# Causal mask of the attention numerators moved from VectorE to ScalarE and GpSimd

## The chip, the cores and the metric

One Trainium2 chip; the kernel runs on one of its NeuronCores. The metric is the device time of one execution in microseconds (us). Every time below is in us from the start of the profiled span unless it says otherwise.

## What is computed

The whole kernel is one decoder block over 16 sequences of 224 tokens with 512 channels: causal self-attention with a rational softmax, cross-attention, and a mixture of experts. The change touches the self-attention alone, of which the reference computes, for 16 heads of 32 channels:

```
scores = q @ k.T * scale - |t - s| * slope[head]
scores = where(s > t, -10000, scores)
num    = 0.5 * (1 + scores * rsqrt(1 + scores * scores))
probs  = num / (sum(num) + 1e-6)
out    = probs @ v
x      = x + out @ w_out.T
```

## The kernel before

Three stages run one after the other: `self_attention`, `cross_attention`, `experts`. Each has its own block in which the five engines (TensorE is `pe`, VectorE `dve`, ScalarE `act`, GpSimd `pool`, SyncE `sp`) run their own instruction lists, held together by semaphores. A stage starts when the one before it has ended on all engines.

`self_attention` works in 8 iterations `i` over two sequences each. An iteration has 8 steps `s`; a step handles four heads of one sequence. The first, the second and the last iteration have bodies of their own ("first", "second", "last"); iterations 2 to 6 are five passes of one loop ("mid"). The order of the work in a step is written out by hand, and so is the table `PLAN` of other products (query, key and value projections Q, K, V of the next sequences, transposes T, output projection OUT, the query projection Z of the next stage) that fill TensorE in each step. The attention itself is pipelined over the steps. In step `s`:

- TensorE issues `scores(s+1)` (L666, L670, L674: four heads, 336 columns each, into the PSUM tile `sc`), then `values(s)` (L691, L694: numerators times v, and numerators times ones, into `pv`), then the step's products. `values(s)` waits for `diag_made`, `off_made` and, as `pv` has one buffer, for `o_made` of the step before.
- ScalarE makes the high part of the last output (`hi_of_output`, L529), then for step `s+1` the square of the scores (L510), the reciprocal root r (L512) and r squared (L514), then the reciprocal of the denominator of step `s` (L522, L524), then copies products out of PSUM, in steps 1 and 2 also normalises 512-channel rows (L476, four instructions), and then `off_diagonal(s+1)` (L518).
- VectorE makes, in this order, the low part of the last output (L383), `product_signed(s+1)` (L360: scores times r), `numerator(s+1)` (L364, L367 and, so far, L369) and `output(s)` (L375, L376, L378, which makes `o_made`), with residual sums and statistics in between.

The numerators of a step lie as four heads by 336 columns on 112 partitions: columns 0 to 223 are the two diagonal blocks (112 keys by 112 queries each), columns 224 to 335 the block below the diagonal, which needs no mask. L367 leaves y there, and the numerator (but for a constant factor) is 2 - y. ScalarE makes 2 - y of the last 112 columns of each head (L518, 448 elements a partition). VectorE makes it of the first 224 (L369, 896 elements) and masks at once, as (y - 2) * keep, where `keep` holds -1 where the query is not before the key and 0 elsewhere:

```
dve.wait_ge(y_made, i * NG + n + 1)
dve.scalar_tensor_tensor(num[n % 2][:, :, 0:2 * R], num[n % 2][:, :, 0:2 * R], 2.0,
                         keep[:, None, :].broadcast_to([R, 4, 2 * R]), ALU.subtract, ALU.mult).then_inc(diag_made, 1)
```

GpSimd fills constants at the start of the stage, `keep` among them, and has nothing to do in it after that. `num` has two buffers.

Of the kernel before, what the change touches and what calls it, by code (L numbers as in the profile page):

```python
# [25 lines left out]
def self_attention(nc, x, w_qkvT, w_outT, w_qT, slopes, x1_dram, q2_dram):  # L26
# [7 lines left out]
    with ExitStack() as ctx:  # L34
# [7 lines left out]
        keep = sb("keep", [R, 2 * R])  # L42
# [63 lines left out]
        diag_made, off_made = sem("diag_made"), sem("off_made")  # L106
        pv_full, rs_made, rden_made, d_made, o_made = sem("pv_full"), sem("rs_made"), sem("rden_made"), sem("d_made"), sem("o_made")
# [78 lines left out]
        CONSTS = 6  # L186
# [69 lines left out]
        def _(pool):  # L256
            pool.memset(ident[:], 1.0).then_inc(const_set, 1)
            pool.memset(keep[:], -1.0).then_inc(const_set, 1)
# [9 lines left out]
            pool.wait_ge(const_set, 11)  # L268
# [3 lines left out]
            for a in range(2):  # L272
                pool.affine_select(out=keep[:, a * R:a * R + R], in_=keep[:, a * R:a * R + R], pattern=[[1, R]],
                                   compare_op=ALU.is_ge, fill=0.0, base=0, channel_multiplier=-1).then_inc(const_ready, 1)
            pool.affine_select(out=head_sel[:], in_=head_sel[:], pattern=[[-6, 4], [-32, 4]], compare_op=ALU.is_ge, fill=0.0,
                               base=0, channel_multiplier=1).then_inc(const_ready, 1)
            pool.wait_ge(const_ready, 4)
# [4 lines left out]
                               base=0, channel_multiplier=1).then_inc(const_ready, 1)  # L282

        @block.vector
        def _(dve):
# [76 lines left out]
            def numerator(i, n):  # L362
                dve.wait_ge(rr_made, i * NG + n + 1)
                dve.scalar_tensor_tensor(u_sb, u_sb, 1.0, q_sb, ALU.add, ALU.mult).then_inc(m_made, 1)  # L364
                dve.wait_ge(p_made, i * NG + n + 1)
                dve.wait_ge(m_made, i * NG + n + 1)
                dve.scalar_tensor_tensor(num[n % 2], u_sb, 3.0, num[n % 2], ALU.subtract, ALU.mult).then_inc(y_made, 1)  # L367
                dve.wait_ge(y_made, i * NG + n + 1)
                dve.scalar_tensor_tensor(num[n % 2][:, :, 0:2 * R], num[n % 2][:, :, 0:2 * R], 2.0,  # L369
                                         keep[:, None, :].broadcast_to([R, 4, 2 * R]), ALU.subtract, ALU.mult).then_inc(diag_made, 1)  # L370
# [97 lines left out]
        def _(act):  # L468
# [47 lines left out]
            def off_diagonal(i, n):  # L516
                act.wait_ge(y_made, i * NG + n + 1)
                act.activation(num[n % 2][:, :, 2 * R:], num[n % 2][:, :, 2 * R:], ACT.Copy, bias=2.0, scale=-1.0).then_inc(off_made, 1)  # L518
# [77 lines left out]
        def _(pe):  # L596
# [81 lines left out]
            def values(i, n):  # L678
                b, g = divmod(n, 4)
                pe.wait_ge(diag_made, i * NG + n + 1)  # L680
                pe.wait_ge(off_made, i * NG + n + 1)
                if not (isinstance(i, int) and i * NG + n == 0):
                    pe.wait_ge(o_made, i * NG + n)
                for den in range(2):
                    for st in range(2):
                        for r in range(4):
                            h = 4 * g + r
                            lhs = ones[:] if den else v[:, 2 * b + st, 32 * h:32 * h + 32]
                            o0 = den * T
                            if st == 0:  # L690
                                mm = pe.matmul(pv[32 * r:32 * r + 32, o0:o0 + T], lhs, num[n % 2][:, r, R:NPAIR],  # L691
                                               start=True, stop=False, tile_position=(0, 32 * r))
                            else:
                                mm = pe.matmul(pv[32 * r:32 * r + 32, o0 + R:o0 + T], lhs, num[n % 2][:, r, 0:R],  # L694
                                               start=False, stop=True, tile_position=(0, 32 * r))
                mm.then_inc(pv_full, 1)
# [1079 lines left out]
```

## Time and profile before

| | us |
|---|---|
| median of 3 runs (lowest, highest) | 3380.05 (3374.13, 3383.58) |
| the profiled execution, its own time | 3391.78 |
| its span, first to last instruction | 3390.1 |
| TensorE busy in the span | 3071.0 (91%) |
| VectorE busy | 1669.1 (49%) |
| ScalarE busy | 1351.4 (40%) |
| GpSimd busy | 732.2 (22%) |
| mean granted TensorE clock | 0.951 |

The profile is of one execution. It took 11.7 us longer than the median run, 1.68 us of which lie around the span. Busy shares are means over three stages with different limits, so they say little on one stage.

### The profile page before, as it was taken

Reading aid. Unit: us, or ns where it says so; the run is one execution under the profiler, and the core shown is the slowest. Engines: PE = TensorE matmul, PEld = TensorE weight load, DVE = VectorE, ACT = ScalarE, POOL = GpSimd, SP = SyncE. Lnnn points to the kernel's source line nnn. Section 1 sums busy time; section 2 is a strip of 40 time slices with the busy share of each in tenths; the row PEclk is TensorE's granted clock in tenths of the full one; section 3 lists DMA queues with packets and bytes.
Section 4 is the critical chain, followed back from the end, with each engine's and each line's share of the span. In section 5 each row is a group of like instructions: output and inputs, shape, how many; then the busy total and the mean of one; then the engine's idle time right before and its main releaser. Section 6 shows DMA issues by size and latency. Waiting matters only on the chain. (4 is left out here: it accounts for less than half of the span.)

```text
span 3390.1 us, 52927 instructions
## 1 busy us (share of the span) xinstructions
PE 3071.0 (91%) x19340; PEld 2500.3 (74%) x19340; DVE 1669.1 (49%) x3816; ACT 1351.4 (40%) x2297; POOL 732.2 (22%) x564
## 2 busy tenths in 40 slices
PE   5889999865999999999999839999999999999997
PEld 4667777754777777777777628887888788878886
DVE  5888888843555565555555623232223232323232
ACT  5677777743555555555555411111111111111111
POOL 0000000001112222121221123333333333333333
PEclk9889999977999999999999859999999999999999
DMA  2011111114111111111110022222222222222222
GB/s 95 23 34 44 43 43 43 44 50 145 37 37 43 36 51 52 36 37 42 48 54 23 17 70 72 61 83 70 74 61 83 70 74 63 81 72 72 66 78 59
DMA packets 96191, 193.80 MB, mean 57 GB/s; under 512 B 18656, under 2 KB 28640, under 8 KB 94016
## 3 DMA queue, kind: packets, MB, share of 16 engines
q1 hardware_dynamic: 80912, 160.78, 15.6%
q0 software_dynamic: 15152, 31.26, 4.4%
q8 instruction: 88, 1.44, 0.2%
q14 instruction: 39, 0.32, 0.0%
HBM read 144.19 MB, written 47.82 MB: 57 GB/s over the span
## 5 line engine op out<-in xcount | busy, mean ns | idle before, releaser
L1619 DVE CAST f_hh<-f_hf 128x448 fp32r<-128x448 f32 x256 | 116.8, 456 | 893.2 <-ACT f_hf L1643 860.5
L1643 ACT ACTIVATE f_hf<-f_h 128x448 f32<-128x448 f32 x256 | 139.6, 545 | 1016.0 <-PE f_h L1679 983.2
L1566 POOL TENSOR_TENSOR f_w1l<-f_raw,f_w1h 128x512 fp32r<-128x512 f32 x130 | 183.4, 1411 | 829.2 <-DVE f_w1h L1601 829.1
L1695 PE MATMUL f_y<-f_w2h,f_hh 128*128 128x512 f32 x896 | 357.9, 399 | 0.0
L1695 PE MATMUL f_y<-f_w2h,f_hl 128*128 128x512 f32 x896 | 354.0, 395 | 0.0
L1695 PE MATMUL f_y<-f_w2l,f_hh 128*128 128x512 f32 x896 | 352.3, 393 | 0.0
L1266 ACT ACTIVATE c_s_sb<-c_s_sb,c_nmx 112x750 f32<-112x750 f32 x256 | 236.0, 922 | 188.9 <-DVE c_nmx L1095 186.5
L1679 PE MATMUL f_h<-f_xTh,f_w1h 128*128 128x448 f32 x1024 | 261.8, 378 | 32.3 <-ACT f_hf L1643 16.8
L1258 ACT COPY c_pT<-c_psum 125x672 f32<-125x672 f32 x256 | 184.7, 722 | 241.1 <-PE c_psum L1359 237.4
L1359 PEld LDWEIGHTS c_psum<-c_ident,c_s_sb 112*125 112x125 f32 x1536 | 198.2, 194 | 90.2 <-issue 84.5
L1679 PE MATMUL f_h<-f_xTl,f_w1h 128*128 128x448 f32 x1024 | 256.1, 373 | 0.0
L1679 PEld LDWEIGHTS f_h<-f_xTh,f_w1h 128*128 128x128 f32 x1024 | 187.9, 190 | 91.0 <-issue 28.2
L1679 PE MATMUL f_h<-f_xTh,f_w1l 128*128 128x448 f32 x1024 | 253.5, 369 | 0.0
L1091 DVE CUSTOM_DVE_ANT_0 c_s_sb<-c_psum,c_mb 112x750 f32<-112x750 f32 x256 | 238.4, 931 | 9.4 <-PE c_psum L1350 9.4
L1359 PE MATMUL c_psum<-c_ident,c_s_sb 112*125 112x112 f32 x1536 | 227.8, 286 | 9.9 <-ACT c_pT L1258 9.3
L1350 PE MATMUL c_psum<-c_kT,c_q 64*112 64x376 f32 x1024 | 207.6, 526 | 21.4 <-DVE c_mx L1091 19.2
L1679 PEld LDWEIGHTS f_h<-f_xTl,f_w1h 128*128 128x128 f32 x1024 | 196.8, 192 | 17.4
L1679 PEld LDWEIGHTS f_h<-f_xTh,f_w1l 128*128 128x128 f32 x1024 | 196.6, 192 | 17.4
L1695 PEld LDWEIGHTS f_y<-f_w2h,f_hl 128*128 128x128 f32 x896 | 168.2, 188 | 39.4
L1695 PEld LDWEIGHTS f_y<-f_w2l,f_hh 128*128 128x128 f32 x896 | 169.0, 189 | 29.7
L1695 PEld LDWEIGHTS f_y<-f_w2h,f_hh 128*128 128x128 f32 x896 | 168.3, 188 | 29.6
L1571 POOL TENSOR_TENSOR f_w2l<-f_raw,f_w2h 128x512 fp32r<-128x512 f32 x130 | 169.9, 1307 | 35.0 <-ACT f_ys L1651 35.0
(243 smaller groups left out, 5725.5 us busy)
## 6 DMA issues: line engine op xcount, KB each, us to landing
f_raw<-in_w SPq DMA_DIRECT2D x132, 512.0 KB
c_craw<-in_ctxT SPq DMA_DIRECT2D x16, 1125.0 KB, 5.1
a_x_in<-in_x SPq DMA_DIRECT2D x9, 896.0 KB, 5.7
a_xr<-in_x SPq DMA_DIRECT2D x8, 896.0 KB, 6.0
x_dram<-a_xr SPq DMA_DIRECT2D x8, 896.0 KB, 4.8
q_dram<-a_q SPq DMA_DIRECT2D x32, 224.0 KB, 5.3
c_q<-q_dram SPq DMA_DIRECT2D x16, 448.0 KB, 5.5
c_x<-x_dram SPq DMA_DIRECT2D x16, 448.0 KB, 4.6
```

Of the source, the lines that this page charges most:

```text
L1091: nc.vector.tensor_tensor_reduce(out=half(s_sb[:, h % 4, :]), in0=score_view(h), in1=half(mb[:]), scale=1.0, scalar=-FLT_MAX, op0=ALU.add, ...
L1258: act.copy(probs_view(h), pt_view).then_inc(p_copied, 1)
L1266: act.activation(s_sb[:, h % 4, :], s_sb[:, h % 4, :], ACT.Exp, bias=nmx[:, h:h + 1], accum_out=den[:, h:h + 1]).then_inc(e_made, 1)
L1350: mm = pe.matmul(scb[e][0:R, a, 0:HW], q[rows, m, t0:t0 + R], kT[rows, m, j0:j0 + HW], start=True, stop=True, tile_position=(64 * e, 0))
L1359: mm = pe.transpose(ptb[0:JB, 128 * j:128 * j + R], s_sb[:, h % 4, JB * j:JB * j + JB], ident[:])
L1566: pool.tensor_tensor(w1s[1][:, n % NSLOT].rearrange("p k c -> p (k c)"), raw1[:, g % 2, n % 2, :], w1s[0][:, n % NSLOT].rearrange("p k c - ...
L1571: pool.tensor_tensor(w2s[1][:, n % NSLOT], raw2[:, g % 2, n % 2, :], w2s[0][:, n % NSLOT].bitcast(F32), ALU.subtract).then_inc(w_lo, 1)
L1619: dve.tensor_copy(hs[0][:, l % 2, c * HC:c * HC + HC], hf[:, c, :]).then_inc(h_hi, 1)
L1643: act.activation(hf[:, c, :], H[:, 0:HC], ACT.Gelu_apprx_tanh).then_inc(free, 1)
L1679: mm = pe.matmul(H[:, 0:HC], w1s[a][:, l % NSLOT, k, :], xT[p][b][:, k, c * HC:c * HC + HC], start=q + k == 0, stop=(q, k) == (2, KC - 1))
L1695: mm = pe.matmul(Y[t][:], hs[a][:, l % 2, 128 * t:128 * t + 128], w2s[b][:, l % NSLOT, :], start=j == 0 and q == 0, stop=j == FB - 1 and q ...
```

## The change

ScalarE makes 2 - y of all columns: `off_diagonal` gets a second instruction ahead of the old one, over the 896 elements of the two diagonal blocks, which raises the new semaphore `two_made`. GpSimd then masks in place, with one affine selection for each diagonal block (448 elements a partition: four heads by 112 queries; entries where the query index is below the partition's key index become 0), and each raises `diag_made`. `values` waits for both. VectorE's L369, with its wait for `y_made`, the tile `keep` and its three set-up instructions on GpSimd are gone. GpSimd also raises a semaphore `two_seen` that nobody waits for.

```diff
-            pool.memset(keep[:], -1.0).then_inc(const_set, 1)
...
-            for a in range(2):
-                pool.affine_select(out=keep[:, a * R:a * R + R], in_=keep[:, a * R:a * R + R], pattern=[[1, R]],
-                                   compare_op=ALU.is_ge, fill=0.0, base=0, channel_multiplier=-1).then_inc(const_ready, 1)
...
+            def diagonal(i, n):
+                pool.wait_ge(two_made, i * NG + n + 1)
+                pool.sem_inc(two_seen, 1)
+                for a in range(2):
+                    block_a = num[n % 2][:, :, a * R:a * R + R]
+                    pool.affine_select(out=block_a, in_=block_a, pattern=[[0, 4], [1, R]], compare_op=ALU.is_ge, fill=0.0,
+                                       base=0, channel_multiplier=-1).then_inc(diag_made, 1)
+
+            diagonal(0, 0)
+
+            def body(i, kind):
+                for s in range(NG):
+                    if has_step(kind, s + 1):
+                        diagonal(*step(i, s + 1))
+
+            iterations(pool, body)
...
                 dve.scalar_tensor_tensor(num[n % 2], u_sb, 3.0, num[n % 2], ALU.subtract, ALU.mult).then_inc(y_made, 1)
-                dve.wait_ge(y_made, i * NG + n + 1)
-                dve.scalar_tensor_tensor(num[n % 2][:, :, 0:2 * R], num[n % 2][:, :, 0:2 * R], 2.0,
-                                         keep[:, None, :].broadcast_to([R, 4, 2 * R]), ALU.subtract, ALU.mult).then_inc(diag_made, 1)
...
             def off_diagonal(i, n):
                 act.wait_ge(y_made, i * NG + n + 1)
+                act.activation(num[n % 2][:, :, 0:2 * R], num[n % 2][:, :, 0:2 * R], ACT.Copy, bias=2.0, scale=-1.0).then_inc(two_made, 1)
                 act.activation(num[n % 2][:, :, 2 * R:], num[n % 2][:, :, 2 * R:], ACT.Copy, bias=2.0, scale=-1.0).then_inc(off_made, 1)
...
-                pe.wait_ge(diag_made, i * NG + n + 1)
+                pe.wait_ge(diag_made, i * (2 * NG) + 2 * n + 2)
```

## Rows read from the trace of the kernel before

**Rows 1.** Windows, stages 1 and 3: length, busy of PE, PEld, DVE, ACT, POOL, clock.

```profile
0.00:767.00 767.00, 637.89 (x5504) 497.87 (x5504) 580.33 (x865) 509.77 (x733) 3.23 (x21) 0.92 0.16 47
...
2000.00:3390.00 1390.00, 1317.86 (x6012) 1112.71 (x6012) 408.78 (x831) 220.28 (x379) 488.95 (x374) 0.98 0.26 71
```

**Rows 2.** Waits from 160 to 720: who waited for whom, total, times, longest.

```profile
DVE a_ew L360 <- ACT a_ew L512: 76.5, 47, 2.3
...
PE a_pv L691 <- DVE a_o_sb L378: 43.2, 17, 7.6
...
PE a_pv L691 <- ACT a_ew L518: 18.3, 6, 3.0
```

**Rows 3.** Timeline of ScalarE and VectorE, step 4 of a mid iteration: start, duration.

```profile
435.52 0.38 ACT L529 CAST a_oTh<-a_o_sb 128x224 fp32r<-128x224 f32 x1 [1.57 <-DVE a_o_sb L378]
...
438.57 1.56 DVE L360 TENSOR_TENSOR a_ew<-a_sc,a_ew 112x1344 f32<-112x1344 f32 x1 [2.25 <-ACT a_ew L512]
...
443.29 0.58 ACT L518 ACTIVATE a_ew<-a_ew 112x448 f32<-112x448 f32 x1 [1.10 <-DVE a_ew L367]
...
443.29 1.09 DVE L369 SCALAR_TENSOR_TENSOR a_ew<-a_ew,a_keep 112x896 f32<-112x896 f32 x1
...
445.44 0.38 ACT L529 CAST a_oTh<-a_o_sb 128x224 fp32r<-128x224 f32 x1 [1.57 <-DVE a_o_sb L378]
```

**Rows 4.** Groups of ScalarE from 80 to 980: busy, mean ns of one.

```profile
L514 ACT ACTIVATE a_ew<-a_ew 112x1344 f32<-112x1344 f32 x61 | 81.1, 1329 | 1.9
...
L518 ACT ACTIVATE a_ew<-a_ew 112x448 f32<-112x448 f32 x61 | 35.1, 576 | 40.5 <-DVE a_ew L367 40.1
```

**Rows 5.** Groups of GpSimd over the whole span.

```profile
L1571 POOL TENSOR_TENSOR f_w2l<-f_raw,f_w2h 128x512 fp32r<-128x512 f32 x130 | 169.9, 1307 | 35.0 <-ACT f_ys L1651 35.0
...
L273 POOL TENSOR_SCALAR_AFFINE_SELECT a_keep<-a_keep 112x112 f32<-112x112 f32 x2 | 0.5, 278 | 0.0
...
L1549 POOL TENSOR_SCALAR_AFFINE_SELECT f_ident<-f_ident 128x128 f32<-128x128 f32 x1 | 0.3, 299 | 0.1
...
L275 POOL TENSOR_SCALAR_AFFINE_SELECT a_head_sel<-a_head_sel 128x16 f32<-128x16 f32 x1 | 0.2, 219 | 0.0
```

**Rows 6.** Timeline of ScalarE, steps 1 to 3 of the same mid iteration.

```profile
413.42 0.56 ACT L518 ACTIVATE a_ew<-a_ew 112x448 f32<-112x448 f32 x1
...
421.89 0.55 ACT L503 ACTIVATE a_q<-a_gen 128x448 f32<-128x448 f32 x1 [1.05 <-PE a_gen L601]
...
425.15 0.56 ACT L518 ACTIVATE a_ew<-a_ew 112x448 f32<-112x448 f32 x1
425.62 0.36 ACT L529 CAST a_oTh<-a_o_sb 128x224 fp32r<-128x224 f32 x1
```

**Rows 7.** Timeline of TensorE, from step 2 of that iteration; in brackets idle before.

```profile
413.56 0.60 PE L620 MATMUL a_tb<-a_ident,a_x_in 112*128 112x112 f32 x4 [0.75 <-ACT a_x_in L476]
...
415.01 0.58 PE L691 MATMUL a_pv<-a_ew,a_v 112*32 112x224 f32 x8
...
425.82 0.98 PE L691 MATMUL a_pv<-a_ew,a_v 112*32 112x224 f32 x8 [3.04 <-ACT a_ew L518]
...
435.63 0.81 PE L691 MATMUL a_pv<-a_ew,a_v 112*32 112x224 f32 x8 [3.01 <-DVE a_o_sb L378]
...
445.55 0.59 PE L691 MATMUL a_pv<-a_ew,a_v 112*32 112x224 f32 x8 [0.28 <-DVE a_o_sb L378]
...
497.98 0.60 PE L620 MATMUL a_tb<-a_ident,a_x_in 112*128 112x112 f32 x4 [0.75 <-ACT a_x_in L476]
```

**Rows 8.** Timeline of TensorE in the first iteration.

```profile
88.74 0.97 PE L691 MATMUL a_pv<-a_ew,a_v 112*32 112x224 f32 x8 [4.38 <-DVE a_o_sb L378]
...
108.58 0.58 PE L691 MATMUL a_pv<-a_ew,a_v 112*32 112x224 f32 x8 [1.52 <-DVE a_o_sb L378]
```

**Rows 9.** Timeline of VectorE and GpSimd in the experts' stage.

```profile
2207.33 2.14 DVE L1619 CAST f_hh<-f_hf 128x448 fp32r<-128x448 f32 x1 [4.02 <-ACT f_hf L1643]
2207.36 1.85 POOL L1571 TENSOR_TENSOR f_w2l<-f_raw,f_w2h 128x512 fp32r<-128x512 f32 x1
```

More of the change, by code:

```diff
@@ L41, in self_attention @@
         ident = sb("ident", [R, R])
-        keep = sb("keep", [R, 2 * R])
         ones = sb("ones", [R, 32])
@@ L106, in self_attention @@
         diag_made, off_made = sem("diag_made"), sem("off_made")
+        two_made, two_seen = sem("two_made"), sem("two_seen")
         pv_full, rs_made, rden_made, d_made, o_made = sem("pv_full"), sem("rs_made"), sem("rden_made"), sem("d_made"), sem("o_made")
@@ L185, in self_attention @@
         stage = lambda n: ew[:, n * 3 * C:(n + 1) * 3 * C]
-        CONSTS = 6
+        CONSTS = 4
         block = ctx.enter_context(nc.Block())
@@ L267, in _ @@
             pool.iota(s_iota, [[1, R]], base=0, channel_multiplier=0, allow_small_or_imprecise_dtypes=True).then_inc(const_set, 1)
-            pool.wait_ge(const_set, 11)
+            pool.wait_ge(const_set, 10)
             pool.affine_select(out=ident[:], in_=ident[:], pattern=[[1, R]], compare_op=ALU.is_equal, fill=0.0,
                                base=0, channel_multiplier=-1).then_inc(const_ready, 1)
-            for a in range(2):
-                pool.affine_select(out=keep[:, a * R:a * R + R], in_=keep[:, a * R:a * R + R], pattern=[[1, R]],
-                                   compare_op=ALU.is_ge, fill=0.0, base=0, channel_multiplier=-1).then_inc(const_ready, 1)
             pool.affine_select(out=head_sel[:], in_=head_sel[:], pattern=[[-6, 4], [-32, 4]], compare_op=ALU.is_ge, fill=0.0,
                                base=0, channel_multiplier=1).then_inc(const_ready, 1)
-            pool.wait_ge(const_ready, 4)
+            pool.wait_ge(const_ready, 2)
             pool.affine_select(out=head_sel[:], in_=head_sel[:], pattern=[[6, 4], [32, 4]], compare_op=ALU.is_ge, fill=0.0,
```

## Prediction

> **What bounds the kernel now.** I read the windows of the three stages first [rows 1]. The change lies in the first, 767 of 3390 us. TensorE is busy for 638 of these, more than VectorE (580) and ScalarE (510), and GpSimd does nothing after its constants. No engine is full, so the order of the work decides. The list of waits says how [rows 2]: VectorE waits for ScalarE's reciprocal root in 47 steps, TensorE waits for VectorE's output (`o_made`) 17 times, 43.2 us, and for ScalarE's L518 six times, 18.3 us. So there are two kinds of wait, and the timeline of one mid iteration shows where each stands.
>
> *The loop between ScalarE and VectorE.* L529 at 435.52 is followed by the square, the root, VectorE's L360, L364 and L367. y is there at 443.29, 7.77 after L529. L518 and L369 start together, then comes `output`, and the next L529 starts at 445.44 [rows 3]. One turn is 9.92 us, of which 2.15 lie between y and L529.
>
> *TensorE.* In the mid iteration `values` waits 3.04, 3.01 and 0.28 us, and from 445.55 TensorE has no idle until the transposes at 497.98, which wait 0.75 for the normalised rows [rows 7]. So over 52 us of an iteration of 84.4 (413.56 to 497.98) TensorE alone sets the pace. The wait of 3.04 is of another kind than the loop: TensorE's Z product ends, ScalarE copies it out (421.89), normalises four rows of blocks, and only then comes L518 (425.15), though y has long been there [rows 6]. `values` starts at 425.82, behind L518. Here ScalarE's queue lies on TensorE's path.
>
> **The change, part by part.**
>
> *Removed.* L369, 1.09 us of VectorE in each of 64 steps. `output` could start right after L367. On GpSimd's set-up three instructions of 0.2 to 0.3 us go; nobody waits for them. VectorE sets the end in none of TensorE's 52 us, so nothing comes back there.
>
> *Added on ScalarE.* 896 elements. L514 takes 1329 ns for 1344 elements, L518 576 ns for 448 [rows 4]: (1329 - 576) / 896 = 0.84 ns an element, so 576 + 448 * 0.84 = 0.95 us. Neighbours on ScalarE overlap by 0.1 (425.15 to 425.62 for 0.56, [rows 6]), so it lengthens the queue by 0.85. It goes ahead of the old L518.
>
> *Added on GpSimd.* Two selections of 448 elements, of which the trace has no like. From 16 elements (219 ns) to 112 (278) is 0.61 ns an element, from 112 to 128 (299) is 1.3 [rows 5]. These give 0.48 and 0.72 us for 448. From above, four selections of 112 are 1.11 and a two-input subtraction of 512 takes 1.31. I take 0.65 each, 1.3 for the pair (0.96 to 2.25), as it is nearest to the selections of the same engine and inner length, with something for the three more rows of the pattern. To this come 0.1 from ScalarE to GpSimd and 0.1 to TensorE, my estimate from the 0.1 between y's maker and the start of its readers and between L518 and `values` (425.71 to 425.82).
>
> The GPSIMD Engine Reference of the Trainium skill (section 4.1) has it that one-input work on GpSimd goes at roughly line rate, and section 3.1 gives 1.8 cycles an element for a tight loop. By my estimate from that page 448 elements are then 0.4 to 0.7 us, and the sum would stay near what the rows give.
>
> *A new turn of the loop.* y at 7.77 after L529. Then ScalarE has 0.85 for the new instruction and 0.47 for L518: the next L529 comes 9.09 after the last. By VectorE alone it would be 9.92 - 1.01 = 8.91 (L369 overlaps its neighbour by 0.08), so ScalarE decides. A turn gains 0.83. But the masked columns are there 7.77 + 0.95 + 0.1 + 1.3 + 0.1 = 10.2 after L529, where `values` now starts 10.1 after it (445.55 for 435.52). So `values` no longer hangs on `o_made` but on GpSimd: it gains nothing in the first turn and 0.83 in each one that follows.
>
> *A mid iteration, steps 2 to 5.* `values` of these steps starts at 415.01, 425.82, 435.63 and 445.55 [rows 7]. The anchor is TensorE's own pace up to step 2.
>
> 1. Step 2. L518 stood at 413.42, right behind a normalisation [rows 6]. The new instruction ends at 414.37, the selections at 415.8 with their waits. `values`, now at 415.01 without idle, starts 0.8 later. Queued behind it is the Z product.
> 2. Step 3. ScalarE's copy of Z (421.89) and the second normalisation come 0.8 later. The new instruction takes L518's place at 425.95, L529 comes at 427.27 instead of 425.62 (+1.65), `values` at 425.95 + 0.95 + 1.5 = 428.4 instead of 425.82 (+2.6).
> 3. Step 4, a loop turn. L529 at 436.36 (before 435.52, +0.84), `values` at 427.27 + 10.2 = 437.5 (+1.9).
> 4. Step 5. `values` at 436.36 + 10.2 = 446.56 (before 445.55): +1.0. TensorE worked 9.92 - 0.28 = 9.64 from 435.63 to 445.55 [rows 7]; with that it would be 437.5 + 9.64 = 447.1, +1.6. In this pass it ran part of it slowly: behind each idle of 3 us the first eight matmuls of `values` take 0.98 and 0.81 us instead of 0.58 [rows 7].
>
> From 445.55 TensorE has no idle, so what is lost is not made up. I take +1.3 a pass, the middle of 1.0 and 1.6. In TensorE's own steps (52.4 us for five, 10.5 each) the square starts as soon as the scores are there, just ahead of `values`, and the masked columns follow 10.2 - 0.3 = 9.9 later (the square starts 0.3 after L529). So 0.6 covers the longer path. With a pair over 1.9 `values` would be late there too, but once a pass and not in each step, since `num` has two buffers and the scores don't wait for `values`. Five passes: +6.5.
>
> *First iteration.* `values` at 88.74 waits 4.38, at 108.58 still 1.52 [rows 8], and between them lie two turns. The first gains nothing (+0.1), the next two 0.83 each: -1.5. After that TensorE sets the pace and the gain stays. *Second:* the delay of step 2 (+0.8), a normalisation behind it that TensorE doesn't wait for, and a turn or two at 0.83, -0.1. *Last:* the normalisation of step 2 and two Z products ahead of the new instruction, +1.8 at its worst by the same walk, then turns that take 0.83 off each, -0.3. Sum: 6.5 - 1.5 - 0.1 - 0.3 = **+4.6, say +5 us**, all in the first stage; the others start when it ends.
>
> *GpSimd beside VectorE.* The trace has a VectorE cast of 0.4 us that took 2.14 beside a GpSimd subtraction and ended 0.26 after it [rows 9]. If VectorE's L383 (two inputs in SBUF), 0.4 after L529's start, is held in that manner until the pair has ended, it is delayed by 0.8. L360 comes 3.05 after L529, behind an idle of 2.25 [rows 3]. I cost it at nothing; that idle is the cover, and without it the loop would grow by up to 0.8 a turn.
>
> SBUF — State Buffer of the Trainium skill, section "Who interferes with whom", speaks against the change: a VectorE instruction with two SBUF inputs and a GpSimd instruction that reads SBUF exclude each other for a whole instruction, whichever starts first. By that rule, the trace agrees, for a cast (2.14 instead of 0.4).
>
> **The rivals.**
>
> 1. *The loop sets the stage (faster).* For: 9.92 us turns and 43 us of waits for `o_made` [rows 2, 3]. If TensorE followed, each of the 26 turns of 9.89 to 9.97 us that the timeline has ([rows 3] is one) would give 0.83: -22 us, 3358. Against: the 52 us without idle, and ScalarE's queue behind the normalisations [rows 6, 7]. It decides where TensorE's apparent work is elastic (the ends of its matmuls are modelled), so that half of these turns count. The chance of more than -10 is 0.11.
> 2. *GpSimd is slow (slower).* Place: between the new ScalarE instruction and `values`. A pair of 2.25 adds 0.95 twice a pass, in step 2, which ScalarE's queue hands on, and in step 5: 5 * 1.9 = 9.5, and some 0.9 in each of the other three iterations: +17 in all, 3397. With +1.6 instead of +1.3 a pass it is +18. It decides over +10, that is from a pair of about 1.7 us, 0.86 a selection. Nothing in the trace excludes it. Chance 0.22.
> 3. *VectorE holds GpSimd (slower, smaller).* If L383 (0.4) slips between the two selections, the pair is 0.4 longer: 5 * 0.8 + 3 * 0.4 = +5 more, about +10, 3390. Against: in rows 9 it is VectorE that is held. Chance 0.12, half of it beyond +10. The page named above, of the Trainium skill, would allow either order.
>
> **How the numbers follow.** The sum stands on the profiled execution, 3391.8, and would make it 3396. The runs' median is 3380.05, 11.7 lower, and other executions should be shifted by the same 5 us: **3385**. Forecast 0.55; rivals 0.11, 0.22, 0.12. Low end: a pair of 0.96 takes 0.34 off 13 times, +0.2, and the clock can give or take about 1.2 a pass (0.4 us for each of the first three of the four groups of `values`, [rows 7]), -6: 3374. High end: rival 2 at +18 and most of such a loss, +4: 3402. 0.3% (10 us) is about what a measurement of this kernel can tell from no change. Faster by more 0.11; within it 0.55 + 0.06 = 0.61; slower by more 0.22 + 0.06 = 0.28.
>
> **What would show it.** Right: mean of the new ScalarE instruction near 0.95 us and of a selection near 0.65; turns of L529 in the first iteration near 9.1; `values` waiting for GpSimd in steps 2 to 5 of a mid iteration; TensorE's idle before `values` of step 3 near 4.7 instead of 3.0; a pass of 85.7 instead of 84.4; stages two and three as long as before. Wrong: selections under 0.5 or over 0.9 us, L367 or L364 longer than 1.56 beside GpSimd, a TensorE idle inside the 52 us, or a pass shorter than 84.

## The result, and the profile after

The changed kernel takes 3388.29 us (median, 3384.45 to 3393.59 of 13 runs), the kernel before beside it on the same chip 3381.76 (3374.13 to 3389.11, 13 runs). The ratio is 1.002, with a 95% interval of 1.0011 to 1.0029: 3.7 to 9.8 us slower. The forecast was +5, 3385 against a range of 3374 to 3402. By the prediction's bound of 0.3% this is no change, though the interval lies above one. Measured again, beside E5 and E6, the same two kernels gave 1.0017 (1.0008 to 1.0026).

The windows of stages one and three in the profile after, with the columns of [rows 1]:

```profile
0.00:767.00 767.00, 635.24 (x5504) 490.27 (x5504) 520.33 (x801) 558.29 (x796) 74.93 (x146) 0.92 0.16 47
...
2000.00:3380.00 1380.00, 1318.16 (x6004) 1113.33 (x6004) 414.44 (x830) 218.94 (x378) 482.92 (x368) 0.98 0.25 70
```

In stage one VectorE's busy time fell by 60 us, ScalarE's rose by 48.5 and GpSimd's by 72. TensorE's is nearly the same (635.24 for 637.89; stage one of the changed kernel ends 3.5 us behind this window). The waits between 160 and 720:

```profile
POOL a_ew L285 <- ACT a_ew L528: 498.8, 53, 12.0
DVE a_ew L373 <- ACT a_ew L522: 88.5, 49, 2.4
...
PE a_pv L702 <- POOL a_ew L285: 69.8, 29, 7.2
DVE a_oTl L393 <- ACT a_oTh L540: 44.3, 28, 3.3
```

L702 is `values` (L691 before), L285 the selections, L528 ScalarE's new instruction, L529 the old `off_diagonal` (L518 before), L540 `hi_of_output` (L529 before), L393 the low part of the output (L383 before). The two rows of [rows 2] in which TensorE waits for `o_made` (43.2 us) and for L518 (18.3), 61.5 together, have become one: it waits for GpSimd 29 times, 69.8 us. The groups of the moved work between 80 and 980:

```profile
L285 POOL TENSOR_SCALAR_AFFINE_SELECT a_ew<-a_ew 112x448 f32<-112x448 f32 x122 | 69.1, 590 | 572.0 <-ACT a_ew L528 572.0
...
L528 ACT ACTIVATE a_ew<-a_ew 112x896 f32<-112x896 f32 x61 | 57.9, 950 | 40.6 <-DVE a_ew L380 40.6
...
L529 ACT ACTIVATE a_ew<-a_ew 112x448 f32<-112x448 f32 x61 | 34.3, 563 | 0.0
...
L393 DVE TENSOR_TENSOR a_oTl<-a_o_sb,a_oTh 128x224 fp32r<-128x224 f32 x62 | 29.9, 483 | 46.2 <-ACT a_oTh L540 45.1 <-issue 1.1
```

ScalarE's instruction is the 950 ns of the forecast; a selection takes 590 ns instead of 650. The mid iteration that answers to [rows 3, 6, 7], steps 2 to 5, on TensorE, ScalarE, GpSimd and VectorE (x8 stands for eight matmuls, x2 for a pair of selections):

```profile
412.67 0.93 ACT L528 ACTIVATE a_ew<-a_ew 112x896 f32<-112x896 f32 x1
...
412.82 0.60 PE L631 MATMUL a_tb<-a_ident,a_x_in 112*128 112x112 f32 x4 [0.71 <-ACT a_x_in L486]
...
413.77 1.11 POOL L285 TENSOR_SCALAR_AFFINE_SELECT a_ew<-a_ew 112x448 f32<-112x448 f32 x2 [12.00 <-ACT a_ew L528]
...
414.94 0.59 PE L702 MATMUL a_pv<-a_ew,a_v 112*32 112x224 f32 x8 [0.60 <-POOL a_ew L285]
...
421.78 0.54 ACT L513 ACTIVATE a_q<-a_gen 128x448 f32<-128x448 f32 x1 [0.92 <-PE a_gen L612]
...
425.04 0.94 ACT L528 ACTIVATE a_ew<-a_ew 112x896 f32<-112x896 f32 x1
...
426.14 1.12 POOL L285 TENSOR_SCALAR_AFFINE_SELECT a_ew<-a_ew 112x448 f32<-112x448 f32 x2 [11.25 <-ACT a_ew L528]
...
426.35 0.36 ACT L540 CAST a_oTh<-a_o_sb 128x224 fp32r<-128x224 f32 x1
...
426.74 0.76 DVE L393 TENSOR_TENSOR a_oTl<-a_o_sb,a_oTh 128x224 fp32r<-128x224 f32 x1 [2.57 <-ACT a_oTh L540]
...
427.31 0.98 PE L702 MATMUL a_pv<-a_ew,a_v 112*32 112x224 f32 x8 [4.65 <-POOL a_ew L285]
...
435.83 0.38 ACT L540 CAST a_oTh<-a_o_sb 128x224 fp32r<-128x224 f32 x1
...
436.81 0.58 PE L702 MATMUL a_pv<-a_ew,a_v 112*32 112x224 f32 x8 [1.96 <-POOL a_ew L285]
...
443.60 0.95 ACT L528 ACTIVATE a_ew<-a_ew 112x896 f32<-112x896 f32 x1 [1.78 <-DVE a_ew L380]
...
444.92 0.36 ACT L540 CAST a_oTh<-a_o_sb 128x224 fp32r<-128x224 f32 x1
...
445.88 0.58 PE L702 MATMUL a_pv<-a_ew,a_v 112*32 112x224 f32 x8 [1.03 <-POOL a_ew L285]
```

To compare kernels, count from the transposes L631 (L620 before) of the same pass, at 412.82 here and 413.56 before. `values` of steps 2, 3, 4 and 5 starts 2.12, 14.49, 23.99 and 33.06 us after them; before it was 1.45, 12.26, 22.07 and 31.99. So step 2 is 0.67 late, step 3 2.23, step 4 1.92, step 5 1.07. L540 turns in 9.48 (426.35 to 435.83) and then in 9.09 (to 444.92) where it turned in 9.92, and still `values` comes later. The turn of 9.48 is longer than the forecast 9.09 because ScalarE first waits 2.20 us for a product of TensorE that stands behind the late `values` of step 3, and copies it, before it comes to L528:

```profile
433.66 0.54 ACT L513 ACTIVATE a_q<-a_gen 128x448 f32<-128x448 f32 x1 [2.20 <-PE a_gen L612]
...
434.51 0.96 ACT L528 ACTIVATE a_ew<-a_ew 112x896 f32<-112x896 f32 x1
```

The next transposes are at 498.34 (before 497.98), so the pass takes 85.52 instead of 84.42: the 1.1 us of step 5, not made up afterwards.

### The profile page after: what moved, and what is told of

Its sections match the earlier page's. It is cut to its first block and busy times, and to the rows that moved or that the text cites. A ratio compares the mean times of both kernels' runs of the same rounds, so it can differ in the third digit from the quotient of the medians.

```text
span 3383.2 us, 53207 instructions
## 1 busy us (share of the span) xinstructions
PE 3062.8 (91%) x19340; PEld 2492.9 (74%) x19340; DVE 1616.0 (48%) x3752; ACT 1399.8 (41%) x2361; POOL 804.2 (24%) x689
## 3 DMA queue, kind: packets, MB, share of 16 engines
q0 software_dynamic: 15152, 31.26, 4.4%
q8 instruction: 88, 1.44, 0.2%
## 5 line engine op out<-in xcount | busy, mean ns | idle before, releaser
L285 POOL TENSOR_SCALAR_AFFINE_SELECT a_ew<-a_ew 112x448 f32<-112x448 f32 x128 | 72.4, 590 | 643.4 <-ACT a_ew L528 643.4
```

Of the source, the lines that this page charges most:

```text
L285: pool.affine_select(out=block_a, in_=block_a, pattern=[[0, 4], [1, R]], compare_op=ALU.is_ge, fill=0.0, base=0, channel_multiplier=-1).th ...
```

## The experiments

E1 to E4 ran together on one chip, E5 and E6 on another together with both kernels again, E7 and E8 together on a third. Each ratio is to runs of the kernel before beside the experiment; on the chip of E1 to E4 that kernel took 3400.74 us and on the others 3382 to 3383, so whole times are compared only as ratios. Stage one does carry over from chip to chip: E4 and E7, the same kernel, end it at 762.0 and 762.3. The table has `values` of steps 2 to 5 in the pass about 410, in us after the transposes, the usual length of a pass, and the end of stage one, which is the time at which GpSimd starts the next stage's constants.

| | 2 | 3 | 4 | 5 | pass | stage one | ratio (95%) |
|---|---|---|---|---|---|---|---|
| before | 1.45 | 12.26 | 22.07 | 31.99 | 84.4 | 767.5 | |
| before, again | 1.45 | 12.20 | 22.02 | 31.95 | 84.3 | 766.5 | |
| after | 2.12 | 14.49 | 23.99 | 33.06 | 85.5 | 770.5 | 1.002 (1.0011-1.0029) |
| after, again | 2.11 | 14.49 | 24.06 | 33.14 | 85.5 | 771.2 | 1.0017 (1.0008-1.0026) |
| E1, no selections | 1.45 | 13.12 | 22.37 | 31.26 | 83.7-84.3 | 761.1 | 0.9996 (0.9981-1.0011) |
| E2, only the removal | 1.45 | 12.18 | 20.87 | 29.67 | 82.0 | 742.7 | 0.9921 (0.9897-0.9944) |
| E3, only ScalarE's load | 1.45 | 13.04 | 22.85 | 32.78 | 85.0-85.2 | 772.5 | 1.0012 (0.9999-1.0026) |
| E4, steps 2, 3 on VectorE | 1.45 | 12.25 | 22.09 | 31.57 | 83.6-83.9 | 762.0 | 0.9996 (0.9981-1.0011) |
| E5, 2 - y on VectorE | 1.45 | 12.28 | 21.98 | 31.44 | 83.9 | 765.6 | 0.9995 (0.9985-1.0005) |
| E6, selections twice | 3.54 | 18.79 | 30.07 | 40.08 | 92.5-94.3 | 826.3 | 1.0183 (1.0166-1.02) |
| E7, E4 again | 1.45 | 12.17 | 22.00 | 31.58 | 83.3-84.0 | 762.3 | 0.9991 (0.9982-1.0) |
| E8, E7 in halves | 1.44 | 12.17 | 21.84 | 31.12 | 83.2-84.8 | 763.7 | 0.9977 (0.9967-0.9986) |

The end of stage one holds a spread that no kernel here explains: E6 apart, TensorE reaches its first `values` between 52.6 and 54.2 us. Counted from there, stage one takes 714.6 and 713.6 us before, 717.4 in both profiles after, and 709.4 and 709.6 in E4 and E7.

**E1. The change without the selections.** The mask is left out.

```diff
-                for a in range(2):
-                    block_a = num[n % 2][:, :, a * R:a * R + R]
-                    pool.affine_select(...).then_inc(diag_made, 1)
...
-                pe.wait_ge(diag_made, i * (2 * NG) + 2 * n + 2)
+                pe.wait_ge(two_made, i * NG + n + 1)
```

> The changed kernel without the two selections (the mask is left out, so later keys count too); TensorE waits for ScalarE's new instruction in their place. Marks, in us after the transposes of normalised rows in a mid pass: values of steps 2, 3, 4, 5 now at 2.12, 14.49, 23.99, 33.06, pass 85.5, first stage ends at 770.5. Theory (TensorE hangs on ScalarE's new instruction and then on GpSimd's pair, each added once in step 2 and once in step 5): step 2 back to 1.45, step 3 at 13.0, step 5 at 31.2, pass 83.7, stage end near 760. Rival (ScalarE's longer queue alone makes the loss, the selections lie beside other work): pass 85 or more, stage end at 769 to 771.

The timeline of TensorE in E1, steps 3 to 5, from its transposes at 408.91:

```profile
422.03 0.98 PE L698 MATMUL a_pv<-a_ew,a_v 112*32 112x224 f32 x8 [3.88 <-ACT a_ew L525]
...
431.28 0.58 PE L698 MATMUL a_pv<-a_ew,a_v 112*32 112x224 f32 x8 [1.67 <-ACT a_ew L525]
...
440.17 0.58 PE L698 MATMUL a_pv<-a_ew,a_v 112*32 112x224 f32 x8 [0.84 <-ACT a_ew L525]
```

TensorE waits for ScalarE's second instruction (L525, the old `off_diagonal` behind the new one). Step 3 is still 0.86 later than before, step 5 0.73 sooner. The selections with their hand-overs are the rest: 1.37 in step 3 (14.49 - 13.12), 1.62 and 1.80 in steps 4 and 5. The pass is 1.2 to 1.8 shorter than after, the stage 9 us (761.1 for the expected 760), so the rival, which had the selections lie beside other work, fell. The whole run shows nothing that its interval can tell from one, so this experiment stands on the passes.

**E2. Only the removal.** The kernel before without L369; 2 - y and the mask of the first 224 columns of each head are left out.

```diff
-                dve.wait_ge(y_made, i * NG + n + 1)
-                dve.scalar_tensor_tensor(num[n % 2][:, :, 0:2 * R], num[n % 2][:, :, 0:2 * R], 2.0,
-                                         keep[:, None, :].broadcast_to([R, 4, 2 * R]), ALU.subtract, ALU.mult).then_inc(diag_made, 1)
...
-                pe.wait_ge(diag_made, i * NG + n + 1)
+                pe.wait_ge(y_made, i * NG + n + 1)
```

> The kernel before without VectorE's mask instruction and with nothing in its place (the 896 elements stay y, unmasked): what the removal alone gives. Theory (the loop gains 1.0 a turn, but step 3 hangs on ScalarE's queue and the steps from 5 on are TensorE's own): step 3 unchanged at 12.26, step 5 at 30 to 30.7 instead of 31.99, pass 82.4 to 83.1 instead of 84.4, stage end near 752 instead of 767.5. Rival (the removal is hidden, TensorE sets the pace everywhere): pass 84.4, stage end 767. Rival (the loop sets the stage): 26 turns and all steps shorter, more than 26 us, stage end below 742.

The timeline of TensorE in E2, from the transposes at 399.21:

```profile
411.39 0.58 PE L688 MATMUL a_pv<-a_ew,a_v 112*32 112x224 f32 x8 [3.04 <-ACT a_ew L515]
...
420.08 0.59 PE L688 MATMUL a_pv<-a_ew,a_v 112*32 112x224 f32 x8 [1.85 <-DVE a_o_sb L375]
...
428.88 0.59 PE L688 MATMUL a_pv<-a_ew,a_v 112*32 112x224 f32 x8 [0.77 <-DVE a_o_sb L375]
```

From `values` to `values` it is 8.80 us (428.88 - 420.08), 1.1 less than before. Step 3 doesn't move (12.18), as it hangs on ScalarE's queue and not on VectorE; steps 4 and 5 gain 1.2 and 2.3. The pass is 2.4 shorter, and the stage 25 us. That is more than I had expected (a pass of 82.4 or more, an end near 752) and hardly short of the 742 at which the rival, the loop that sets the stage, was to be taken as true. It isn't by the rival's way, though: step 3 doesn't move, and from step 5 to the next transposes it is 52.3 us as before (82.0 - 29.67; 84.42 - 31.99 = 52.4). The rest lies outside the later mid passes: the second iteration, 79.9 from transposes to transposes where it was 83.6, gains more than a mid pass. The whole run is 22 us shorter (3378.59 for 3400.74, by the interval 19 to 35). So L369's time is worth much in this stage, if nothing takes its place. With the mask gone the later stages work on other data, which may bear on the whole run and doesn't on the passes.

**E3. Only ScalarE's load.** The kernel before, with the new instruction writing its 896 elements into a spare tile.

```diff
                 act.wait_ge(y_made, i * NG + n + 1)
+                act.activation(q_sb[:, :, 0:2 * R], r_sb[:, :, 0:2 * R], ACT.Copy, bias=2.0, scale=-1.0)
                 act.activation(num[n % 2][:, :, 2 * R:], num[n % 2][:, :, 2 * R:], ACT.Copy, bias=2.0, scale=-1.0).then_inc(off_made, 1)
```

> The kernel before with one more ScalarE instruction of 896 elements ahead of the old one, into a tile that is dead by then; its result is not used. VectorE still masks. Theory (ScalarE's queue behind the normalisations is on TensorE's path): steps 3, 4, 5 later by 0.85 each (13.1, 22.9, 32.8), pass 85.2 instead of 84.4, stage end near 772; loop turns stay at 9.92. Rival (GpSimd alone makes the loss): pass 84.4, stage end 767.5.

As expected: 0.78 us later in step 3 and no more in steps 4 and 5, and the pass 0.6 to 0.8 longer. The idle ahead of step 3 grows from 3.04 [rows 7] to 3.88, in E1 too:

```profile
428.77 0.97 PE L692 MATMUL a_pv<-a_ew,a_v 112*32 112x224 f32 x8 [3.88 <-ACT a_ew L519]
```

The queue behind the normalisation is a cost on its own, paid once a pass, and the stage is 5 us longer (1.1 of them ahead of the first `values`). The whole run's interval, 0.9999 to 1.0026, just holds one. The first mid pass is an exception: it takes 85.06 us here and 86.01 in the kernel before, for which see the part on the sum.

**E4. The other version.** VectorE keeps the masking in steps 2 and 3, where ScalarE has a normalisation ahead; the other six steps are as changed. The edit against the changed kernel, in the lists of GpSimd, VectorE and ScalarE (the counts that GpSimd and TensorE wait for change with it):

```diff
+        ON_DVE = (2, 3)
...
+                if n in ON_DVE:
+                    return
...
+                if n in ON_DVE:
+                    dve.wait_ge(y_made, i * NG + n + 1)
+                    dve.scalar_tensor_tensor(num[n % 2][:, :, 0:2 * R], num[n % 2][:, :, 0:2 * R], 2.0,
+                                             keep[:, None, :].broadcast_to([R, 4, 2 * R]), ALU.subtract, ALU.mult).then_inc(diag_dve, 1)
...
-                act.activation(num[n % 2][:, :, 0:2 * R], ...).then_inc(two_made, 1)
+                if n not in ON_DVE:
+                    act.activation(num[n % 2][:, :, 0:2 * R], ...).then_inc(two_made, 1)
```

> The changed kernel, but the numerators of steps 2 and 3 of each iteration, which stand behind the normalisations in ScalarE's queue, are masked by VectorE as before. Theory: steps 2 and 3 back at 1.45 and 12.26, step 4 at 22.1, step 5 at 31.2 to 31.8 (before 31.99, changed 33.06), pass 83.6 to 84.2, stage end near 762.5, which is faster than both kernels, by some 5 us against before. Rival (the loss comes in all steps alike): pass 85 or more, stage end 769 or more.

Steps 2 and 3 are back at 1.45 and 12.25, step 5 is 0.42 sooner than before, and stage one ends at 762.0, 5 us before both profiles of the kernel before and 8 to 9 before those of the changed one. The rival, a loss in all steps alike, fell. The whole run's interval (0.9981 to 1.0011) holds one, and also the 0.9985 that 5 us would make.

**E5. 2 - y of the masked columns on VectorE.** ScalarE has only its old instruction, GpSimd masks.

```diff
+                dve.wait_ge(y_made, i * NG + n + 1)
+                dve.tensor_scalar(num[n % 2][:, :, 0:2 * R], num[n % 2][:, :, 0:2 * R], -1.0, 2.0, ALU.mult, ALU.add).then_inc(two_made, 1)
...
-                act.activation(num[n % 2][:, :, 0:2 * R], num[n % 2][:, :, 0:2 * R], ACT.Copy, bias=2.0, scale=-1.0).then_inc(two_made, 1)
```

> VectorE makes 2 - y of the 896 elements without the mask (one tensor input, constants), GpSimd masks as in the changed kernel, ScalarE has its old queue again. Theory: steps 2 and 3 back at 1.45 and 12.26. If VectorE's new instruction is faster than its old one (0.62 us) and nothing holds it, a loop turn is 9.45, step 5 at 31.2, pass 83.6, stage end near 762. Rival (GpSimd's selections now run beside VectorE's output, whose last instruction reads two SBUF tiles and is held until the pair ends): a turn of about 10.1 instead of 9.92, step 5 at 32.4, pass 84.8, stage end near 770.

VectorE, and under it GpSimd, in step 5 of E5:

```profile
441.53 0.63 DVE L382 TENSOR_SCALAR a_ew<-a_ew 112x896 f32<-112x896 f32 x1
...
442.79 0.39 DVE L390 SCALAR_TENSOR_TENSOR a_o_sb<-a_dt 128x224 f32<-128x224 f32 x1
```

```profile
442.32 1.30 POOL L285 TENSOR_SCALAR_AFFINE_SELECT a_ew<-a_ew 112x448 f32<-112x448 f32 x2 [8.16 <-DVE a_ew L382]
```

And the pair of step 4 of the same pass, with each selection by itself, beside the same VectorE instruction:

```profile
433.33 0.39 DVE L390 SCALAR_TENSOR_TENSOR a_o_sb<-a_dt 128x224 f32<-128x224 f32 x1
```

```profile
432.87 0.58 POOL L285 TENSOR_SCALAR_AFFINE_SELECT a_ew<-a_ew 112x448 f32<-112x448 f32 x1 [9.41 <-DVE a_ew L382]
433.40 0.77 POOL L285 TENSOR_SCALAR_AFFINE_SELECT a_ew<-a_ew 112x448 f32<-112x448 f32 x1
```

The same 896 elements cost VectorE 0.63 us here and 1.09 in L369 [rows 3], which also reads `keep`. Step 3 is at its old place again: with ScalarE's queue untouched the delay of step 3 is gone, which is E3 the other way round. The rival (the pair holds VectorE's `output`, turns of 10.1) fell: L390, which reads two SBUF tiles, took 0.39 as ever, and it was the pair that took 1.30 instead of 1.11. The turn is the 9.45 of the theory (433.76 to 443.22 for L541, `hi_of_output`), but its sizes were missed: step 5 at 31.44 for 31.2, a pass of 83.9 for 83.6, and the stage ends at 765.6 for 762, only 1 to 2 us ahead of the kernel before. The whole run's interval holds one.

**E6. Each selection twice.** One cost doubled, the rest as changed.

```diff
-                for a in range(2):
+                for q, a in enumerate((0, 1, 0, 1)):
+                    if q == 2:
+                        pool.wait_ge(diag_made, i * (4 * NG) + 4 * n + 2)
+                        pool.sem_inc(two_seen, 1)
...
-                pe.wait_ge(diag_made, i * (2 * NG) + 2 * n + 2)
+                pe.wait_ge(diag_made, i * (4 * NG) + 4 * n + 4)
```

> The changed kernel with each pair of selections made twice (the second finds nothing left to do): the pair's time goes from 1.1 to about 2.35 us. Theory: step 2 at 3.4 instead of 2.12, step 3 at 17.0 instead of 14.49, step 5 at 35.5 instead of 33.06, pass 88.0 instead of 85.5, and in TensorE's own steps up to 0.5 more once; stage end near 786 instead of 770.5. Rival (the selections are hidden beside other work in most steps): pass under 86.5.

Step 2 came as worked out (3.54 for 3.4), the rest did not: step 3 at 18.79 for 17.0, step 5 at 40.08 for 35.5, a pass of 92.5 to 94.3 for 88.0, and stage one ends 40 us later than the 786 expected. The rival, selections that are hidden beside other work, fell. TensorE in E6, from the transposes at 439.54:

```profile
443.08 0.59 PE L705 MATMUL a_pv<-a_ew,a_v 112*32 112x224 f32 x8 [2.03 <-POOL a_ew L288]
...
458.33 0.97 PE L705 MATMUL a_pv<-a_ew,a_v 112*32 112x224 f32 x8 [5.92 <-POOL a_ew L288]
...
469.61 0.58 PE L705 MATMUL a_pv<-a_ew,a_v 112*32 112x224 f32 x8 [3.24 <-POOL a_ew L288]
```

And the windows behind steps 2 and 3 in E6, then behind the same two steps in the changed kernel; the seventh number is the granted clock:

```profile
443.00:451.40 8.40, 8.32 (x60) 6.77 (x60) 6.23 (x8) 4.59 (x7) 0.03 (x1) 0.80 0.00 0
458.30:465.40 7.10, 7.07 (x51) 5.42 (x51) 5.57 (x6) 3.17 (x5) 0.00 (x0) 0.57 0.43 132
```

```profile
414.90:421.70 6.80, 6.76 (x64) 5.67 (x64) 4.60 (x5) 5.87 (x9) 0.00 (x0) 1.00 0.00 0
427.30:433.90 6.60, 6.59 (x52) 5.04 (x52) 4.62 (x4) 4.30 (x6) 0.00 (x0) 0.63 0.62 201
```

Behind an idle of 2.03 us instead of 0.60 TensorE's work of step 2 took 1.6 us more, at a clock of 0.80 instead of 1.00. That is nearly all of the 1.8 by which step 3 missed its 17.0. From the start of these `values` to the end of the step's work, the same 80 matmuls take 9.33 us for 7.72. A further 1.28 us in the pair of each step makes the pass 7 to 9 us longer, where my own sum had 2.5. Of the 8.8 us in this pass, TensorE's busy time has 3.7 (80.25 for 76.58) and its idle time 5.1 (14.09 for 8.94). So the clock is less than half of it. The rest is waiting that comes again in nearly every step, in those that TensorE had for itself too:

```profile
479.29 1.29 ACT L523 ACTIVATE a_ew<-a_sc 112x1344 f32<-112x1344 f32 x1 [1.54 <-PE a_sc L688]
```

```profile
490.50 0.59 PE L705 MATMUL a_pv<-a_ew,a_v 112*32 112x224 f32 x8 [0.34 <-POOL a_ew L288]
```

TensorE's list has the scores of the next step behind `values` and its products. When `values` waits for the selections, the scores come later, ScalarE's square waits for them (1.54 us here), and with it the numerators and selections that the next `values` waits for.

**The two kernels again.**

> The changed kernel again, in the same call as the others, for the noise of the other stages. Theory (all of the change lies in the first stage): stage end at 770 to 771, stages two and three as long as in the kernel before within their own spread, ratio near 1.001. Rival (the change also lengthens the later stages): ratio at or over 1.002, and stages two and three longer in both profiles of the changed kernel than in those of before.

> The kernel before again, for a second profile: stage end at 767 to 768; what stages two and three differ by from the first profile (2622.6 us) is the noise of those stages.

The passes repeat to 0.2 us. The end of stage one differs by 4.8 us in this pair of profiles and by 3.0 in the first. Stages two and three together take 2622.6 us before and 2612.7 after, and again 2613.1 and 2613.3. So they are not longer with the change in both pairs, and the rival fell, though the ratio, 1.0017, lies nearer to its 1.002 than to the theory's 1.001. The kernel before ended stage one at 766.5, half a microsecond ahead of what was expected.

**E7. E4 again.** The same kernel on another chip.

> The kernel of e4_steps23_vector once more, beside the kernel before in five rounds: VectorE masks the numerators of steps 2 and 3 as before, the other six steps are those of the change. Theory (ScalarE's queue behind the two normalisations is what costs, and the loop turn of 9.1 us instead of 9.9 is what gives): the first stage ends at 762 us as in e4 (before 766.5 to 767.5), the whole is 5 us shorter than before, a ratio of 0.9985. Rival (five microseconds of the first stage are given back later, by the clock or otherwise): stage one again 5 us shorter, the whole at 1.000.

Stage one ends at 762.3. 3378.48 us (11 runs) for 3382.05 (20 runs), a ratio of 0.9991: the interval ends at 1.0, with the theory's 0.9985 inside it and the rival's 1.000 at its end. Against the changed kernel this interval is clear (to 1.0 here, from 1.0008 and 1.0011 there), while that of E4 itself was wider and reached 1.0011; against the kernel before it is likely and not settled. The loop no longer sets step 5 in the pass about 410: TensorE works without idle from `values` of step 4 to those of step 5, 9.58 us at a granted clock of 0.82.

**E8. E7 with ScalarE's instruction in two halves.** GpSimd starts on the first diagonal block while ScalarE makes the second.

```diff
-                pool.wait_ge(two_made, ...)
-                pool.sem_inc(two_seen, 1)
                 for a in range(2):
+                    pool.wait_ge(two_made, (i * (NG - len(ON_DVE)) + n - sum(m < n for m in ON_DVE)) * 2 + a + 1)
+                    pool.sem_inc(two_seen, 1)
...
-                    act.activation(num[n % 2][:, :, 0:2 * R], ...).then_inc(two_made, 1)
+                    for a in range(2):
+                        block_a = num[n % 2][:, :, a * R:a * R + R]
+                        act.activation(block_a, block_a, ACT.Copy, bias=2.0, scale=-1.0).then_inc(two_made, 1)
```

> As e7_steps23_again, but where ScalarE and GpSimd make the masked columns, ScalarE does it in two instructions of 448 elements, one for each diagonal block, and GpSimd starts its first selection behind the first of them. Theory (values hangs on the sum of ScalarE's instruction and the pair): second block ready on ScalarE 1.04 after y (0.56 + 0.48) instead of 0.95, its selection 0.1 + 0.58 later, 1.7 after y instead of 2.15. values of steps 4 and 5 starts 0.35 to 0.45 sooner, step 5 at 31.2 us after the transposes instead of 31.6, the pass 83.3 instead of 83.7, stage one 759 to 760. Rival (the longer queue of ScalarE, 0.1 a turn, and two more hand-overs eat it): step 5 at 31.6, stage one at 762 or later.

ScalarE, GpSimd and TensorE in step 5 of the pass about 410:

```profile
440.54 1.04 ACT L543 ACTIVATE a_ew<-a_ew 112x448 f32<-112x448 f32 x2 [1.78 <-DVE a_ew L388]
...
441.28 1.23 POOL L293 TENSOR_SCALAR_AFFINE_SELECT a_ew<-a_ew 112x448 f32<-112x448 f32 x2 [8.05 <-ACT a_ew L543]
...
442.56 0.59 PE L720 MATMUL a_pv<-a_ew,a_v 112*32 112x224 f32 x8 [1.21 <-POOL a_ew L293]
```

From the start of ScalarE's work to `values` it is 2.02 us (440.54 to 442.56); in the changed kernel 2.28 (443.60 to 445.88). Step 5 starts at 31.12, as the theory had it (31.2). The overlap gave 0.26 in this place instead of the 0.35 to 0.45 expected, with the pair at 1.23 for 1.11. Against E7, step 5 is 0.46 sooner, and the overlap isn't all of that: step 4 is 0.16 sooner, and from there to step 5 the granted clock was 1.00, with 8.07 us of work and 1.21 of idle, where E7 had 9.58 us of work at 0.82. Three of the four passes from 243 on take 83.2 to 83.6, one 84.8: there TensorE worked at a granted clock of 0.71 between steps 4 and 5. So stage one ended at 763.7 in the profiled execution and not at 759 to 760, which is on the rival's side (762 or later) and no sooner than in E7. The whole run is 3374.82 us (10 runs) for 3382.05, 0.9977 (0.9967 to 0.9986): by its interval 4.7 to 11.2 us faster than the kernel before, and clear of the changed one. It overlaps E7's interval (0.9982 to 1.0), so what halving alone gives the whole run is not settled. Stage one of this profile is 2.8 to 3.8 shorter than in the two of before; where the rest of the median's 7.2 us lies, one profile doesn't show.

## Why the prediction was right

**ScalarE's instruction.** 0.95 from 0.84 ns an element; 950 ns in 61 instances. Its 0.85 of queue, too: L529 starts 0.84 behind it (425.04, 425.88), and E3 adds 0.78 to step 3 and nothing to the turns.

**The selections.** 1.3 for the pair; it was 1.11. It lay between the bounds, 0.96 to 2.25, and nearer to the lower, which comes from the slope between 16 and 112 elements [rows 5]: of the 0.34 that I had put on top of it, 0.15 was needed. By the estimate from the GPSIMD Engine Reference of the Trainium skill (sections 3.1 and 4.1) it was to be 0.4 to 0.7; the trace agrees, with 0.59.

**The hand-overs.** 0.1 and 0.1: L528 ends at 413.60 and the pair starts at 413.77, 0.17 later; it ends at 414.88 and `values` starts at 414.94, 0.06 later. The 10.1 from L529 to `values` of the kernel before is 10.0 (445.55 - 435.52 = 10.03), which would make the loss of the first turn +0.2 instead of +0.1.

**The walk through a mid pass.** Step 2 +0.67 for +0.8, step 3 +2.23 for +2.6, step 4 +1.92 for +1.9, step 5 +1.07 for +1.0 to +1.6. The steps' causes are those named: `values` waits for GpSimd in all four, and 4.65 us in step 3 for the forecast of 4.7. That step 4 came out to a tenth is partly luck: step 3 was 0.4 less late than forecast, and the turn behind it took 9.48 instead of 9.09, since ScalarE waited for TensorE's product. The term taken, +1.3, was 0.2 too large, as the lower end (the turn of the loop) decided and not TensorE's own 9.64 us, and the pair is shorter. The turn from step 4 to step 5 was 9.09 for 9.09; in the first iteration 9.07.

**First, second, last.** The transposes that open the second iteration come 1.19 sooner in the first pair of profiles (158.41 for 159.60; forecast -1.5) and 0.2 later in the second pair (159.44 for 159.24). The two agree when they are taken apart. From the first transposes inside the first iteration (77.49 and 77.96; again 77.13 and 79.04) to these it is 1.66 and 1.71 less, the turns of the forecast. Ahead of them lies a loss that the prediction did not have: the second `values` comes 13.89 and 13.84 us behind the first instead of 13.07, +0.8. E3 has 13.88 there, so ScalarE's load alone makes it. And in the second pair the first `values` itself comes 1.04 later (53.89 for 52.85), in the first pair 0.13. From the second iteration's transposes to those of the first mid pass it is -0.5 and -0.2 (forecast -0.1). From the fifth mid pass's transposes to the end of the stage it is +1.45 and +0.95, of which one pass takes 1.1: +0.35 and -0.15 for the last iteration (forecast -0.3).

**The sum.** The term of the five mid passes, +6.5, is the one that was mis-sized, for a cause that I had named for the range only, the clock. Of the five mid passes the first gained nothing: transposes to transposes 86.01 and 85.82 (again: 85.84 and 85.88), though its step 5 is 1.4 late there too. The windows of TensorE's work behind that step, before and after:

```profile
275.19:287.24 12.05, 12.05 (x92) 9.57 (x92) 9.94 (x14) 7.29 (x11) 0.00 (x0) 0.86 0.01 2
```

```profile
274.88:285.36 10.48, 10.48 (x92) 8.35 (x92) 7.73 (x11) 7.02 (x11) 1.11 (x2) 1.00 0.10 29
```

The same 92 matmuls took 12.05 us at a granted clock of 0.86 before (12.03 at 0.86 in the other profile), and 10.48 at 1.00 after (10.42 at 1.00). The other kernels show that neither the selections nor the shorter turn is needed for this. E3 has only ScalarE's load added, and the same idle ahead of this step as before (1.90 us for 1.88), and its window reads:

```profile
278.25:288.62 10.37, 10.37 (x92) 8.46 (x92) 9.22 (x13) 8.12 (x12) 0.00 (x0) 1.00 0.03 9
```

In all ten profiles other than the two of the kernel before this stretch has 10.4 to 10.6 us of work at 1.00. What decides it is open. The trace of the kernel before had a hint, its first mid pass of 86.01 us, but the forecast took the pass about 410 for all five. So four passes at 1.1 (1.2 to 1.4 in the second pair) and one at 0 give 4.4 to 5 instead of 6.5. All in all stage one ends 3.0 us later in one pair of profiles and 4.8 in the other, for a sum of +4.6, and the timed runs say 3.7 to 9.8. That the sum came so near is in part luck, as the mid passes' term was some 2 too large, and the 0.8 of the second `values`, a last iteration above its -0.3 and, in the second pair, the late start of the stage made up for it.

**The rivals.** *The loop sets the stage* fell: turns did shorten, by 0.83 between steps 4 and 5, and `values` came later all the same. E2 shows that it was no idle thought: with nothing in L369's place the stage is 25 us shorter. *GpSimd is slow* fell at 1.11, under its 1.7. E6 shows that its price was put too low: with 2.4 from the first start to the last end (1.11 + 0.16 + 1.11) the run is 60 us longer than before, where the prediction's sum would give 19. The step that failed in it is that the scores don't wait for `values`, so that a slow pair would cost only once a pass in TensorE's own steps. They stand behind `values` in TensorE's list, and `values` waited for GpSimd in seven of the eight steps of the pass in E6. The clock behind the longer idles is the smaller part. *VectorE holds GpSimd* fell in the changed kernel: L393 is the one held, 0.76 instead of 0.38 in steps 3 and 4, with the pair at 1.12 and 1.11; where it starts later than the pair's end (446.37 in step 5) it takes 0.38. The idle ahead of L373, 1.88 us there, covers it, as costed. The cast of [rows 9], which the prediction put beside this, has one input in SBUF and is no case of two. Seven pairs of stage one took 1.26 instead of 1.11: in those VectorE's L388 (two inputs in SBUF) starts ahead of the second selection, so the rival does happen, with L388 and not L393, and at 0.15 us.

**Stages two and three.** From 2000 on, stage three is as busy as before ([rows 1] and the window above). From the end of stage one to the start of stage three it is 1223.6 us before and 1210.6 after, but again 1213.9 and 1214.3. So one profile of each doesn't show what the change does there, and the whole spans (3390.1, 3383.2) would have told the wrong sign. Stage one's own end and the timed runs are what can be compared.

## What to carry to other kernels

When work is moved to another engine, price two things apart: what the loop's turn gains, and what stands in the receiving engine's queue at that place. Here the same 0.95 us on ScalarE made `values` late where a normalisation lay ahead and nowhere else (E3), so choosing the engine by step (E4) turned a loss into a stage shorter by 4 to 5 us. Cutting the moved work in two so that both engines overlap (E8) took 0.26 us off the way to `values`, and that kernel is the only complete one here whose whole time is clearly below that of the kernel before, though not below E7's. A receiving engine's queue also holds waits for others: a late `values` makes TensorE's products and scores late, ScalarE stands for them, and the delay goes round once more (E6). A removal measured alone (E2) tells what is to be had before the replacement is built.

## What the runs showed of the hardware

**Idle time of TensorE costs more than itself.** In E6 1.28 us more in each pair made a pass 7 to 9 us longer, of which 1.9 to 3.7 are longer busy time of TensorE (78.34 to 80.25 us for 76.5), with the granted clock at 0.80 and 0.57 behind steps 2 and 3 where it was 1.00 and 0.63, that is, with more of the stretch at 1.2 GHz instead of 2.4. The idle just ahead doesn't settle the clock by itself: behind 1.88 us the same 92 matmuls ran at 0.86 in the kernel before, and behind 1.90 us at 1.00 in E3, a difference of 1.7 us (12.05 - 10.37).

**Who holds whom between VectorE and GpSimd goes by who starts first.** Beside a pair of selections VectorE's L393 (two inputs in SBUF), which starts at 426.74, 0.07 behind the second selection of its pair, took 0.76 us for 0.38, and the pair kept its 1.12. In E5, L390 started 0.47 behind the pair's start, took its 0.39, and the pair took 1.30. The section "Who interferes with whom" of the page SBUF — State Buffer (Trainium skill) has two-input VectorE instructions and GpSimd exclude each other for a whole instruction: the trace agrees in who is held, for L393, and in E5 as well, in step 4, where L390 starts 0.07 ahead of the second selection (433.33 and 433.40) and that one takes 0.77 for 0.58, while the first keeps its 0.58. How much is less than a whole instruction there: 0.19 us, for an L390 of 0.39.

**What the same 896 elements cost on VectorE.** L369, a `scalar_tensor_tensor` with `keep` as second input, takes 1.09 us, L382 of E5, a `tensor_scalar` without it, 0.63. The two differ in kind as well as in inputs, and no run here tells these apart.
